# The closing stage of a mixer-and-experts kernel: its first load in two transfers, its last chunk finished in two halves

## The chip, the cores and the metric

The kernel runs on one core of one Trainium2 chip. The metric is the time of one execution on the device in microseconds (us), taken as the median of several runs. Profile views give times from the start of the span, which is the part of an execution that the profiler records.

## What is computed

One transformer-like layer on 4 x 1024 tokens of 256 values, in float32. First a sequence mixer with a residual, then a mixture of eight experts (two of them for each token, and a shared one), whose output is normalised and added to the mixer's result:

```python
x = x + _layernorm(attn_ref(_layernorm(x), ...))      # call the result x1
...
for e in range(E):
    out = out + comb[:, e:e + 1] * _swiglu(xn, gate_up_w[e], down_w[e])
out = out + _swiglu(xn, shared_gate_up_w, shared_down_w)
...
x = x + _layernorm(out)                               # x1 + normalised sums
```

The change concerns the last line only: for each of 4096 tokens, subtract the mean of its 256 sums, divide by the root of the variance plus 1e-5, and add x1.

## The kernel before

The mixer runs first, in `mixer`. It leaves three things in device memory: x1 in `x1_scratch`, each token's normalised row, sorted by expert, in `xs_scratch`, and the shared expert's output in `acc_scratch`. Then `experts` works through 39 groups of up to 256 token rows. For each group TensorE multiplies with the weights of its expert, which SyncE loads chunk by chunk, and GpSimd adds the results to `acc_scratch` with indirect DMAs that accumulate (L1271). When the last of these has landed, the closing stage begins. The expert phase takes most of the time; the closing stage starts at about 1162 of the span's 1199.7 us.

The closing stage handles the 4096 tokens in `NC` = 8 chunks of `TC` = 4 tiles of 128 tokens (512 KB each). The tiles `acc[c]` lie in buffers that the earlier stages no longer use: `xnt` for chunks 0 to 4, `x_in` for 5 and 6, and `s` for 7. The small statistics lie in `xr`. The work on a chunk passes through five engines in order:

- SyncE loads chunk after chunk from `acc_scratch` (L1255), all eight issues one behind the other.
- VectorE (`moments_of`) takes the statistics of the four tiles (`bn_stats`, L1462), aggregates them (L1467), and prepares the negative mean and the variance (L1470, L1471).
- GpSimd (`root`) raises the variance to the power of -1/2 and multiplies (L1281, L1283).
- ScalarE normalises each tile in place (L1396).
- Even chunks are stored by GpSimd with a DMA that adds to x1, which was copied into `out` before (`add_out`, L1289). For odd chunks VectorE adds x1 from on-chip memory (`add_x1`, L1477), and SyncE stores the sum (L1259).

The order on each engine is the order of the code. On VectorE, the x1 addition of an odd chunk comes two chunks late, so that its wait is short; that of chunk 7 comes last. On GpSimd, `add_out` of chunk c-2 comes behind `root(c)`, so the store of chunk 6 follows the root of chunk 7. SyncE waits for the loads' issue, then for `sum_ready` once for each odd chunk, and in the end for all stores, its own and GpSimd's:

```python
for c in range(1, NC, 2):
    sp.wait_ge(sum_ready, c // 2 + 1)
    sp.dma_start(token_rows(out)[c, :, :, :], acc[c]).then_inc(sum_stored, 16)
sp.wait_ge(sum_stored, 16 * (NC // 2))
sp.wait_ge(out_added, 16 * (NC // 2))
```

The semaphore `acc_loaded[c]` says that chunk c is loaded, and `normed` counts the chunks that ScalarE has normalised. SyncE's DMAs go through queue q1 (hardware_dynamic), GpSimd's through q0 (software_dynamic); both use the same 16 DMA engines.

Of the kernel before, what the change touches and what calls it, by code (L numbers as in the profile page):

```python
# [7 lines left out]
ALU = mybir.AluOpType  # L8
# [4 lines left out]
P = 128  # L13
# [1134 lines left out]
TC = 4  # L1148
NC = TT // TC


def token_rows(dram):

    return dram.rearrange("b l d -> (b l) d").rearrange("(c t p) d -> c p t d", t=TC, p=P)


def experts(nc, ctx, w_s, xs_dram, acc_dram, x1_dram, out, group_expert, group_change, group_row, group_code, vec, ident, neg_half,
# [5 lines left out]
    def sem(name):  # L1163
        return ctx.enter_context(nc.semaphore(name))

    LAG = 3
    w, rows, xg_hi, xg_lo, xg_f, gate, hg_hi, hg_lo, y, acc, x1, small = homes
# [9 lines left out]
    acc_loaded = [sem(f"f_loaded{c}") for c in range(NC)]  # L1177
    order, aggregated, moments = sem("f_order"), sem("f_aggregated"), sem("f_moments")
    rooted, rs_ready, normed = sem("f_rooted"), sem("f_rs_ready"), sem("f_normed")
    x1_moved, out_added = sem("x1_moved"), sem("out_added")  # L1180
    sum_ready, sum_stored = sem("sum_ready"), sem("sum_stored")

    gu_ps, down_ps, x_ps = banks[0:2], [banks[2:4], banks[4:6]], banks[6]
    loaded = [sem(f"chunk_loaded{f}") for f in range(FC)]
# [7 lines left out]
    def groups(eng, turn):  # L1192

        turn(0, 0)
        with eng.Fori(0, (NG - 1) // 2) as i:
            for k in range(2):
                turn(i * 2 + 1 + k, 1 - k)
# [3 lines left out]
    def sync(sp):  # L1201
        def load_rows(g, par):
            row = sp.value_load(group_row[0:1, bass.ds(g, 1)], min_val=0, max_val=SPARE)
            sp.dma_start(rows[:, par, :, :], xs_dram[bass.ds(row, G), :].rearrange("(t p) d -> p t d", p=P)
                         ).then_inc(rows_loaded[par], 16)

        def load_chunk(g, f, e, new):
            sp.wait_ge(down_done, g * FC + f + 1)
            sp.dma_start(w[f].bitcast(F32), w_s[e, f, :, :], cond=new).then_inc(loaded[f], 16)

        def turn(g, par):
            e = sp.value_load(group_expert[0:1, bass.ds(g, 1)], min_val=0, max_val=E - 1)
            new = sp.value_load(group_change[0:1, bass.ds(g, 1)], min_val=0, max_val=1)
            for f in range(FC):
                load_chunk(g, f, e, new)
                if f == 1:
                    if not (isinstance(g, int) and g == 0):
                        sp.wait_ge(x_turned, g * DC + DC)
                        sp.wait_ge(meta_ready, g)
                    load_rows(g + 1, 1 - par)  # L1220

        def first_rows(b, par=0):
            row = sp.value_load(star[0:1, 1 + par:2 + par], min_val=0, max_val=SPARE)
            sp.dma_start(rows[:, par, :, :], xs_dram[bass.ds(row, G), :].rearrange("(t p) d -> p t d", p=P)
                         ).then_inc(rows_loaded[par], 16)

        def first_weights():
            e = sp.value_load(star[0:1, 0:1], min_val=0, max_val=E - 1)
            for f in range(FC):
                sp.dma_start(w[f].bitcast(F32), w_s[e, f, :, :]).then_inc(loaded[f], 16)  # L1230

        def others():
            def move_x1(c):
                if c % 2 == 0:
                    sp.dma_start(token_rows(out)[c, :, :, :], token_rows(x1_dram)[c, :, :, :]).then_inc(x1_moved, 16)
                else:
                    sp.dma_start(x1[c // 2], token_rows(x1_dram)[c, :, :, :]).then_inc(x1_moved, 16)

            sp.wait_ge(x_turned, 2 * DC)
            sp.wait_ge(meta_ready, 1)  # L1240
            load_rows(2, 0)
            free(sp, "x1")
            move_x1(0)
            for c in range(1, NC):
                turn(c + 1, 1 - c % 2)
                move_x1(c)
            with sp.Fori(0, (NG - 1 - NC) // 2) as i:
                for k in range(2):
                    turn(i * 2 + NC + 1 + k, 1 - k)
            for par in range(2):  # L1250
                sp.wait_ge(rows_loaded[par], 16 * (NG // 2 + 1))
            for par in range(2):
                sp.wait_ge(y_added[par], 16 * GT * ((NG + 1 - par) // 2))
            for c in range(NC):
                sp.dma_start(acc[c], acc_dram[c * TC * P:(c + 1) * TC * P, :].rearrange("(t p) d -> p t d", p=P)  # L1255
                             ).then_inc(acc_loaded[c], 16)
            for c in range(1, NC, 2):
                sp.wait_ge(sum_ready, c // 2 + 1)
                sp.dma_start(token_rows(out)[c, :, :, :], acc[c]).then_inc(sum_stored, 16)  # L1259
            sp.wait_ge(sum_stored, 16 * (NC // 2))  # L1260
            sp.wait_ge(out_added, 16 * (NC // 2))
        return first_rows, first_weights, others

# [97 lines left out]
    def scalar(act):  # L1361
        def rows_hi(g, par, c):
            act.wait_ge(x_turned, g * DC + c + 1)
            nc.scalar.activation(xg_hi[:, par, c, :], x_ps[:, 0:G], ACT.Identity,
                                 bias=vec[:, V_BE + c:V_BE + c + 1],
                                 scale=vec[:, V_G + c:V_G + c + 1]).then_inc(x_hi_ready, 1)
            nc.scalar.activation(xg_f[:, c, :], x_ps[:, 0:G], ACT.Identity,
                                 bias=vec[:, V_BE + c:V_BE + c + 1],
                                 scale=vec[:, V_G + c:V_G + c + 1]).then_inc(x_f_ready, 1)

        def h_high(g, f):
            act.wait_ge(h_ready, g * FC + f + 1 + 2)
            nc.scalar.activation(hg_hi[:, f % 4, :], gate[:, f % 4, :], ACT.Copy).then_inc(h_hi_ready, 1)  # L1373
        def turn(g, par):
            for f in range(FC):
                if f >= 1:
                    h_high(g, f - 1)
                elif not (isinstance(g, int) and g == 0):
                    h_high(g - 1, FC - 1)
                act.wait_ge(clipped, g * FC + f + 1)  # L1380
                nc.scalar.activation(gate[:, f % 4, :], gate[:, f % 4, :], ACT.Silu).then_inc(silu_ready, 1)  # L1381
                if f in (2, 5):
                    rows_hi(g + 1, 1 - par, (f - 2) // 3)
        def first_hi(b, c):
            if c == 0:
                free(act, "xg")
            rows_hi(0, 0, c)

        def rest():
            act.sem_inc(down_done, FC)  # L1390
            groups(act, turn)
            h_high(NG - 1, FC - 1)
            for c in range(NC):
                act.wait_ge(rs_ready, c + 1)
                for t in range(TC):
                    i = nc.scalar.activation(acc[c][:, t, :], acc[c][:, t, :], ACT.Identity, bias=nm[:, c, t:t + 1],  # L1396
                                             scale=rs[:, c, t:t + 1])
                i.then_inc(normed, 1)
        return first_hi, rest

    def vector(dve):
# [52 lines left out]
        def rest():  # L1454
            free(dve, "gate")
            groups(dve, turn)
            h_low(NG - 1, FC - 1)
            copy_y(NG - 1, 0)
            def moments_of(c):
                dve.wait_ge(acc_loaded[c], 16)  # L1460
                for t in range(TC):
                    i = nc.vector.bn_stats(st[:, c, t, :], acc[c][:, t, :])  # L1462
                i.then_inc(order, 1)
                dve.wait_ge(order, c + 1)
                dve.sem_inc(seen, 1)
                for t in range(TC):
                    i = nc.vector.bn_aggr(mv[:, c, t, :], st[:, c, t, :])  # L1467
                i.then_inc(aggregated, 1)
                dve.wait_ge(aggregated, c + 1)
                nc.vector.tensor_scalar(mv[:, c, :, 0], mv[:, c, :, 0], -1.0, None, ALU.mult)  # L1470
                nc.vector.tensor_scalar(ve[:, c, :], mv[:, c, :, 1], 1.0, EPS, ALU.mult, ALU.add).then_inc(moments, 1)  # L1471

            def add_x1(c):
                if c == 1:
                    dve.wait_ge(x1_moved, 16 * NC)
                dve.wait_ge(normed, c + 1)
                nc.vector.tensor_tensor(acc[c], acc[c], x1[c // 2], ALU.add).then_inc(sum_ready, 1)  # L1477

            for c in range(NC):
                moments_of(c)  # L1480
                if c % 2 == 1 and c > 1:
                    add_x1(c - 2)
            add_x1(NC - 1)
        return seeds, first_lo, rest

    return sync, gpsimd, tensor, scalar, vector
# [69 lines left out]
```

## Time and profile before

| | us |
|---|---|
| median of 3 runs | 1206.18 |
| lowest and highest | 1205.74 and 1206.53 |
| the profiled execution, its own time | 1201.74 |
| its span | 1199.7 |
| TensorE busy in the span | 1106.7 (92%) |
| VectorE busy | 828.7 (69%) |
| ScalarE busy | 654.8 (55%) |
| GpSimd busy | 307.5 (26%) |

The profiled execution is one execution by itself, and what a view says of durations holds for it. Its time lies 2.0 us above its span and 4.4 us below the median of the runs. Busy shares are of the whole span, most of which is the mixer and the experts; the closing stage, where TensorE does nothing, must be read in stretches of its own.

### The profile page before, as it was taken

The numbers are of one execution on the slowest core, as the hardware profiler recorded it, in microseconds if no ns is written. First come the engines' busy times: TensorE is split into PE (matmuls) and PEld (weight loads), VectorE is DVE, ScalarE is ACT, GpSimd is POOL, SyncE is SP. The second block draws the span as 40 slices with busy tenths as digits, with TensorE's granted clock in tenths as the row PEclk, the third lists the DMA queues.
The fourth block names the chain that finished last, engine by engine and source line by source line (L and its number), as shares of the span: only waits on it lengthen the run. The fifth ranks groups of instructions, "written<-read, shape, count | busy, mean of one in ns | idle before, by whom it ended". The sixth has DMA issues, their size and how long they took to land.

```text
span 1199.7 us, 23250 instructions
## 1 busy us (share of the span) xinstructions
PE 1106.7 (92%) x7492; PEld 981.8 (82%) x7492; DVE 828.7 (69%) x2089; ACT 654.8 (55%) x1304; POOL 307.5 (26%) x358
## 2 busy tenths in 40 slices
PE   4899899999989999999999999999999999999950
PEld 2665676676677567999999999999999999999940
DVE  4896888798797666666666666666666666666645
ACT  6777768677685354444444444444444444444425
POOL 2032032722542634121221122112112211221225
PEclk9899999999999999999999999999999999999985
DMA  8657675875675678532231245555912356211239
GB/s 275 224 195 235 224 226 191 271 256 175 231 248 174 212 246 339 147 70 54 53 70 20 33 137 184 187 173 180 367 33 35 77 202 229 35 25 28 35 79 219
DMA packets 96617, 191.70 MB, mean 160 GB/s; under 512 B 8768, under 2 KB 59456, under 8 KB 96576
## 3 DMA queue, kind: packets, MB, share of 16 engines
q1 hardware_dynamic: 80160, 170.38, 41.8%
q0 software_dynamic: 16416, 20.85, 10.2%
q8 instruction: 17, 0.28, 0.1%
q14 instruction: 24, 0.20, 0.1%
HBM read 295.62 MB, written 86.41 MB: 318 GB/s over the span
## 4 chain that ended last, share of the span: by engine, by line
PE 81%; DVE 5%; ACT 4%; issue 4%; DMA 3%; POOL 3%; SPq 1%; ACTq 0%; DVEq 0%; POOLq 0%
PE bank L1321 12%; PE bank L1322 12%; PE bank L1323 12%; PE bank L457 11%; PE bank L1334 6%; PE bank L1332 6%; PE bank L1333 6%; PE bank L451 4%; PE bank L453 4%; PE bank L452 4%; POOL xs_scratch L1128 2%; PE bank L1309 1%; DMA xs_scratch<-n,slot_now 1%; DVE xr L1462 1%; PE bank L468 1%
## 5 line engine op out<-in xcount | busy, mean ns | idle before, releaser
L1271 POOL DMA_INDIRECT acc_scratch<-cv,ids x78 | 128.2, 1644 | 559.6 <-DVE cv L1410 518.6
L1321 PE MATMUL bank<-h_hi,w_both 128*128 128x256 f32 x936 | 269.9, 288 | 0.4 <-DVE cv L1438 0.4
L1431 DVE TENSOR_SCALAR cv<-bank 128x256 f32<-128x256 f32 x312 | 132.2, 424 | 198.7 <-PE bank L1323 197.9
L1322 PE MATMUL bank<-h_hi,w_both 128*128 128x256 f32 x936 | 262.9, 281 | 0.0
L1323 PE MATMUL bank<-h_hi,w_both 128*128 128x256 f32 x936 | 262.2, 280 | 0.0
L1381 ACT ACTIVATE cv<-cv 128x256 f32<-128x256 f32 x312 | 130.3, 418 | 241.4 <-DVE cv L1431 240.4
L1373 ACT ACTIVATE h_hi<-cv 128x256 fp32r<-128x256 f32 x312 | 129.7, 416 | 115.0 <-DVE cv L1438 115.0
L1321 PEld LDWEIGHTS bank<-h_hi,w_both 128*128 128x128 f32 x936 | 176.5, 189 | 0.7 <-issue 0.7
L1323 PEld LDWEIGHTS bank<-h_hi,w_both 128*128 128x128 f32 x936 | 176.8, 189 | 0.0
L1322 PEld LDWEIGHTS bank<-h_hi,w_both 128*128 128x128 f32 x936 | 176.5, 189 | 0.0
L1438 DVE TENSOR_TENSOR cv<-bank,cv 128x256 f32<-128x256 f32 x312 | 132.5, 425 | 46.9 <-ACT cv L1381 40.2
L1333 PE MATMUL bank<-w_both,h_hi 128*128 128x256 f32 x468 | 132.0, 282 | 0.0
L1334 PE MATMUL bank<-w_both,h_hi 128*128 128x256 f32 x468 | 131.9, 282 | 0.0
L1332 PE MATMUL bank<-w_both,h_hi 128*128 128x256 f32 x468 | 131.8, 282 | 0.0
L1426 DVE TENSOR_TENSOR h_hi<-cv,h_hi 128x256 fp32r<-128x256 f32 x312 | 130.2, 417 | 0.8 <-ACT h_hi L1373 0.6
L451 PE MATMUL bank<-xs_hi,w_both 128*128 128x512 f32 x224 | 99.2, 443 | 17.7 <-DVE xs_lo L825 10.4
L1111 POOL TENSOR_TENSOR h_lo<-h,h_hi 128x512 fp32r<-128x512 f32 x32 | 47.3, 1483 | 171.7 <-ACT h_hi L706 171.7
L453 PE MATMUL bank<-xs_hi,w_both 128*128 128x512 f32 x224 | 90.4, 404 | 0.0
L452 PE MATMUL bank<-xs_lo,w_both 128*128 128x512 f32 x224 | 90.4, 404 | 0.0
L1334 PEld LDWEIGHTS bank<-w_both,h_hi 128*128 128x128 f32 x468 | 88.4, 189 | 0.0
L1333 PEld LDWEIGHTS bank<-w_both,h_hi 128*128 128x128 f32 x468 | 88.1, 188 | 0.0
L1332 PEld LDWEIGHTS bank<-w_both,h_hi 128*128 128x128 f32 x468 | 87.8, 188 | 0.0
(227 smaller groups left out, 2405.3 us busy)
## 6 DMA issues: line engine op xcount, KB each, us to landing
w_both<-w_split SPq DMA_DIRECT2D x228, 768.0 KB
xs_hi<-w_split SPq DMA_DIRECT2D x38, 768.0 KB
xs_lo<-w_split SPq DMA_DIRECT2D x38, 768.0 KB
e_raw<-w_e SPq DMA_DIRECT2D x64, 384.0 KB
w_split<-e_high SPq DMA_DIRECT2D x64, 384.0 KB
w_split<-e_raw SPq DMA_DIRECT2D x64, 384.0 KB
u<-xs_scratch SPq DMA_DIRECT2D x40, 260.0 KB, 3.4
x_in<-x SPq DMA_DIRECT2D x8, 512.0 KB, 5.6
```

The source lines that it names most:

```text
L451: nc.tensor.matmul(out, hi, x_hi, start=first, stop=False)
L452: nc.tensor.matmul(out, hi, x_lo, start=False, stop=False)
L453: return nc.tensor.matmul(out, lo, x_hi, start=False, stop=last)
L457: return nc.tensor.matmul(out, w, x, start=first, stop=last)
L1321: nc.tensor.matmul(out, e_hi[f][:, cols], xg_hi[:, par, c, :], start=c == 0, stop=False)
L1322: nc.tensor.matmul(out, e_hi[f][:, cols], xg_lo[:, par, c, :], start=False, stop=False)
L1323: i = nc.tensor.matmul(out, e_lo[f][:, cols], xg_hi[:, par, c, :], start=False, stop=c == DC - 1)
L1332: nc.tensor.matmul(out, hg_hi[:, f % 4, toks], e_hi[f][:, 4 * P:CW], start=f == 0, stop=False)
L1333: nc.tensor.matmul(out, hg_hi[:, f % 4, toks], e_lo[f][:, 4 * P:CW], start=False, stop=False)
L1334: i = nc.tensor.matmul(out, hg_lo[:, f % 4, toks], e_hi[f][:, 4 * P:CW], start=False, stop=f == FC - 1)
L1431: nc.vector.tensor_scalar(gate[:, f % 4, :], gu_ps[f % 2][:, 0:G], CLIP, -CLIP, ALU.min, ALU.max).then_inc(clipped, 1)
L1438: nc.vector.tensor_tensor(gate[:, f % 4, :], gu_ps[f % 2][:, G:2 * G], gate[:, f % 4, :], ALU.mult).then_inc(h_ready, 1)
```

## The change

The first load becomes two transfers of 256 KB, each for two of the four tiles. The first one signals a new semaphore, `acc_half_loaded`, the second one `acc_loaded[0]`. VectorE starts on the first two tiles after the first signal and waits for the second ahead of the third tile. On the last chunk, ScalarE also signals `normed` after its second tile; VectorE adds x1 to two tiles at a time, and SyncE stores each half when it is ready. The other six chunks, and the statistics and roots of all, are as before.

```diff
--- before.py
+++ after.py
@@ -1179,6 +1179,8 @@
     rooted, rs_ready, normed = sem("f_rooted"), sem("f_rs_ready"), sem("f_normed")
     x1_moved, out_added = sem("x1_moved"), sem("out_added")
     sum_ready, sum_stored = sem("sum_ready"), sem("sum_stored")
+    acc_half_loaded = sem("acc_half_loaded")
+    TH = TC // 2
 
     gu_ps, down_ps, x_ps = banks[0:2], [banks[2:4], banks[4:6]], banks[6]
     loaded = [sem(f"chunk_loaded{f}") for f in range(FC)]
@@ -1251,13 +1253,20 @@
                 sp.wait_ge(rows_loaded[par], 16 * (NG // 2 + 1))
             for par in range(2):
                 sp.wait_ge(y_added[par], 16 * GT * ((NG + 1 - par) // 2))
-            for c in range(NC):
+            first_rows_of_acc = acc_dram[0:TC * P, :].rearrange("(t p) d -> p t d", p=P)
+            sp.dma_start(acc[0][:, 0:TH, :], first_rows_of_acc[:, 0:TH, :]).then_inc(acc_half_loaded, 16)
+            sp.dma_start(acc[0][:, TH:TC, :], first_rows_of_acc[:, TH:TC, :]).then_inc(acc_loaded[0], 16)
+            for c in range(1, NC):
                 sp.dma_start(acc[c], acc_dram[c * TC * P:(c + 1) * TC * P, :].rearrange("(t p) d -> p t d", p=P)
                              ).then_inc(acc_loaded[c], 16)
-            for c in range(1, NC, 2):
+            for c in range(1, NC - 1, 2):
                 sp.wait_ge(sum_ready, c // 2 + 1)
                 sp.dma_start(token_rows(out)[c, :, :, :], acc[c]).then_inc(sum_stored, 16)
-            sp.wait_ge(sum_stored, 16 * (NC // 2))
+            for h in range(2):
+                half = slice(h * TH, (h + 1) * TH)
+                sp.wait_ge(sum_ready, NC // 2 + h)
+                sp.dma_start(token_rows(out)[NC - 1, :, half, :], acc[NC - 1][:, half, :]).then_inc(sum_stored, 16)
+            sp.wait_ge(sum_stored, 16 * (NC // 2 + 1))
             sp.wait_ge(out_added, 16 * (NC // 2))
         return first_rows, first_weights, others
 
@@ -1395,6 +1404,8 @@
                 for t in range(TC):
                     i = nc.scalar.activation(acc[c][:, t, :], acc[c][:, t, :], ACT.Identity, bias=nm[:, c, t:t + 1],
                                              scale=rs[:, c, t:t + 1])
+                    if c == NC - 1 and t == TH - 1:
+                        i.then_inc(normed, 1)
                 i.then_inc(normed, 1)
         return first_hi, rest
 
@@ -1457,8 +1468,10 @@
             h_low(NG - 1, FC - 1)
             copy_y(NG - 1, 0)
             def moments_of(c):
-                dve.wait_ge(acc_loaded[c], 16)
+                dve.wait_ge(acc_half_loaded if c == 0 else acc_loaded[c], 16)
                 for t in range(TC):
+                    if c == 0 and t == TH:
+                        dve.wait_ge(acc_loaded[0], 16)
                     i = nc.vector.bn_stats(st[:, c, t, :], acc[c][:, t, :])
                 i.then_inc(order, 1)
                 dve.wait_ge(order, c + 1)
@@ -1480,7 +1493,11 @@
                 moments_of(c)
                 if c % 2 == 1 and c > 1:
                     add_x1(c - 2)
-            add_x1(NC - 1)
+            for h in range(2):
+                half = slice(h * TH, (h + 1) * TH)
+                dve.wait_ge(normed, NC + h)
+                nc.vector.tensor_tensor(acc[NC - 1][:, half, :], acc[NC - 1][:, half, :], x1[NC // 2 - 1][:, half, :],
+                                        ALU.add).then_inc(sum_ready, 1)
         return seeds, first_lo, rest
 
     return sync, gpsimd, tensor, scalar, vector
```

On SyncE, the closing stage before. The first row waits for everything ahead of the stage; the last waits for all stores.

```order
L1255 DMA xnt<-acc_scratch 128x4x256 [waits y_added0,y_added1,x_rows_loaded1,x_rows_loaded0]
L1255 DMA xnt<-acc_scratch 128x4x256 x4
L1255 DMA x_in<-acc_scratch 128x4x256 x2
L1255 DMA s<-acc_scratch 128x4x256
L1259 DMA out<-xnt 128x4x256 [waits sum_ready] x2
L1259 DMA out<-x_in 128x4x256 [waits sum_ready]
L1259 DMA out<-s 128x4x256 [waits sum_ready]
L64 UNCONDITIONAL_BRANCH [waits out_added,sum_stored]
```

And on SyncE now:

```order
L1257 DMA xnt<-acc_scratch 128x2x256 [waits y_added0,y_added1,x_rows_loaded1,x_rows_loaded0]
L1258 DMA xnt<-acc_scratch 128x2x256
L1260 DMA xnt<-acc_scratch 128x4x256 x4
L1260 DMA x_in<-acc_scratch 128x4x256 x2
L1260 DMA s<-acc_scratch 128x4x256
L1264 DMA out<-xnt 128x4x256 [waits sum_ready] x2
L1264 DMA out<-x_in 128x4x256 [waits sum_ready]
L1268 DMA out<-s 128x2x256 [waits sum_ready] x2
L64 UNCONDITIONAL_BRANCH [waits out_added,sum_stored]
```

There is one more load ahead of the seven that follow, and one more store at the end; all the others keep their places.

On VectorE, the first chunk of the stage before, behind the last two results of the experts (L1410):

```order
L1410 TENSOR_SCALAR cv<-bank,share 128x256
L1462 BN_STATS xr<-xnt 128x6 [waits f_loaded0]
L1462 BN_STATS xr<-xnt 128x6 x3
L1467 BN_AGGR xr<-xr 128x2 [waits f_order]
L1467 BN_AGGR xr<-xr 128x2 x3
```

The same place now:

```order
L1421 TENSOR_SCALAR cv<-bank,share 128x256
L1475 BN_STATS xr<-xnt 128x6 [waits acc_half_loaded]
L1475 BN_STATS xr<-xnt 128x6
L1475 BN_STATS xr<-xnt 128x6 [waits f_loaded0]
L1475 BN_STATS xr<-xnt 128x6
L1480 BN_AGGR xr<-xr 128x2 [waits f_order]
L1480 BN_AGGR xr<-xr 128x2 x3
```

The four statistics have two waits instead of one. At the end of the stage, VectorE's last row `L1477 TENSOR_TENSOR` on 128x1024 values has become two of `L1499` on 128x512, each with a wait for `normed`. No instruction of ScalarE or GpSimd has moved.

## Rows read from the trace of the kernel before

**Rows 1.** Chain of waits that ended last, stretch 1140:1200 (start us, us, what)

```profile
1162.64 4.14 DMA xnt<-acc_scratch
```

**Rows 2.** Timeline, stretch 1150:1200 (start us, us, engine, line, operation [idle before, releaser])

```profile
1166.81 1.41 DVE L1462 BATCH_NORM_STATS2 xr<-xnt 128x6 f32<-128x256 f32 x4 [10.79 <-DMA xnt<-acc_scratch]
...
1168.91 1.40 DVE L1462 BATCH_NORM_STATS2 xr<-xnt 128x6 f32<-128x256 f32 x4
...
1185.30 1.34 POOL L1289 DMA_DIRECT2D out<-xnt  x1
...
1186.24 0.39 DVE L1471 TENSOR_SCALAR xr<-xr 128x4 f32<-128x4 f32 x1
...
1187.56 0.37 SPq L1259 DMA_DIRECT2D out<-x_in  x1
...
1188.72 1.34 POOL L1289 DMA_DIRECT2D out<-x_in  x1
1188.73 2.07 ACT L1396 ACTIVATE s<-s,xr 128x256 f32<-128x256 f32 x4 [1.34 <-POOL xr L1283]
1190.84 1.23 DVE L1477 TENSOR_TENSOR s<-s,e_high 128x1024 f32<-128x1024 f32 x1 [3.31 <-ACT s L1396]
1192.09 0.37 SPq L1259 DMA_DIRECT2D out<-s  x1
```

**Rows 3.** DMA queues (packets, MB, share), the five stretches that the prediction names, in order

```profile
q1 hardware_dynamic: 4072, 4.04, 108.6%
...
q0 software_dynamic: 334, 0.34, 113.2%
...
q1 hardware_dynamic: 188, 0.19, 108.1%
...
q0 software_dynamic: 322, 0.33, 114.1%
...
q1 hardware_dynamic: 373, 0.37, 69.0%
```

**Rows 4.** Times to landing, lines L1289, L1259: chunks 3, 4, 5, 6, 7, by start

```profile
L1259 SPq DMA_DIRECT2D out<-xnt x1: 378/378/378, 1181.8 to 1181.8; - x1
...
DMA to landing us min/median/max: 6.3/6.3/6.3
...
DMA to landing us min/median/max: 6.0/6.0/6.0
...
DMA to landing us min/median/max: 5.4/5.4/5.4
...
DMA to landing us min/median/max: 7.0/7.0/7.0
...
DMA to landing us min/median/max: 5.0/5.0/5.0
```

**Rows 5.** Line L64, the program's end: the drains of GpSimd and SyncE

```profile
L64 POOLq DRAIN  x1: 10741/10741/10741, 1188.7 to 1188.7; - x1
...
L64 SPq DRAIN  x1: 7/7/7, 1197.2 to 1197.2; - x1
```

**Rows 6.** Line L1255, load of chunk 1; line L1396, chunk 7 (ns, start us)

```profile
L1255 SPq DMA_DIRECT2D xnt<-acc_scratch x1: 501/501/501, 1163.1 to 1163.1; - x1
...
DMA to landing us min/median/max: 5.2/5.2/5.2
...
L1396 ACT ACTIVATE s<-s,xr x4: 585/586/600, 1188.7 to 1190.2; 128x256 f32<-128x256 f32 x4
```

**Rows 7.** Queue, stretch 1162.6:1165; then stretches: busy by engine, clock, DMA share, GB/s

```profile
q1 hardware_dynamic: 137, 0.14, 35.3%
...
1165.25:1165.50 0.25, 0.00 (x0) 0.00 (x0) 0.00 (x0) 0.00 (x0) 0.00 (x0) 0.50 1.10 393
...
1188.00:1188.50 0.50, 0.00 (x0) 0.00 (x0) 0.00 (x0) 0.00 (x0) 0.42 (x2) 0.50 0.93 121
1188.50:1189.00 0.50, 0.00 (x0) 0.00 (x0) 0.00 (x0) 0.27 (x1) 0.48 (x2) 0.50 1.15 184
```

## Prediction

> **What bounds the closing stage.** I read three views. First the chain of waits that ended last [rows 1]: the stage began with a 4.14 us wait for the first 512 KB load of the sums, and from there the chain ran over VectorE. Then the timeline [rows 2], which shows why: VectorE started the statistics of chunk 0 at 1166.81, those of chunk 1 at 1168.91, and worked through all eight chunks nearly without a pause, to 1186.63 (the 0.39 us instruction that began at 1186.24). It waits for data only once, the 10.79 us ahead of chunk 0. So what chunk 0 gains, the rows behind it can gain too, as far as their own loads have landed.
>
> After 1186.63 the page's chain goes GpSimd root, ScalarE normalising, VectorE add, SyncE store, and stops at the add that ends at 1192.07. The span is 1199.7. What fills the 7.6 us in between is in neither view; it has to be read from the queues [rows 3]. There each queue has a stretch to itself. In 1188.0:1190.0 all 334 packets are on q0 (GpSimd's accumulating stores), in 1191:1191.5 all 188 are on q1 (SyncE's plain stores), in 1192.6:1194.4 all 322 are on q0 again, and in 1195.5:1197 all 373 are on q1. With the landings [rows 4] this gives an order. Chunk 4 (GpSimd, issued 1185.30, 6.0 us) landed at 1191.3; chunk 5 (SyncE, 1187.56, 5.4) at 1192.9; chunk 6 (GpSimd, 1188.72, 7.0) at 1195.7; chunk 7 (SyncE, 1192.09, 5.0) at 1197.1. The engines serve one store, then the next, and the last four are a backlog: chunk 5, issued at 1187.56, moved nothing in 1188.0:1190.0, and chunk 7, issued at 1192.09, moved nothing in 1192.6:1194.4. **The end of the kernel hangs on the DMA engines, not on the last add.** What feeds this backlog is the issue of chunk 4 at 1185.30.
>
> Behind that lies one more step [rows 5]: GpSimd's closing drain began at 1188.7 and took 10741 ns, so it ended at 1199.5, about 3.8 us after chunk 6 landed and 2.4 us after chunk 7 landed; SyncE's own drain took 7 ns, at 1197.2. The program ends when GpSimd's drain does. That the last plain store is on the end path is therefore not even certain.
>
> **Part 1, the first load in two transfers.** SyncE issues one more load; the one for chunk 1 took 0.50 us [rows 6]. The loads behind it come up to 0.5 us later to the queue but not later to the engines: from 1165 on, q1 moved 4072 packets of about 1 KB by 1176.5 at 351 GB/s [rows 3], so the bytes, not the issues, set when each load lands. I cost the issue at nothing; if that cover is gone, it costs its 0.5 us. Of the 512 packets of chunk 0, the second 256 take 262 KB / 393 GB/s = 0.67 us by the rate at which the stream ran in 1165.25:1165.50 [rows 7]. So the first half should land 0.67 us earlier, at 1166.1 instead of 1166.78. VectorE then does two of the four statistics (1.41 / 4 each, 0.71 together) while the rest lands, and the aggregates come 0.7 earlier. Now what is late next: the load of chunk 1, issued at 1163.1, landed 5.2 us later [rows 6], at 1168.3. VectorE could now ask for it at 1168.2 and waits until about 1168.32, against 1168.91 before. **Gain 0.59 us.** Chunk 2's load follows by 512 KB / 351 GB/s = 1.5 us, at 1169.8, well ahead of 1168.32 + 2.1 (the distance of the two rows of statistics) = 1170.4, when VectorE asks for it. Bounds: 0, if the two half transfers do not land in order; 0.71, if the stream itself starts sooner because its first transfer is shorter (from 1162.6 to 1165 only 137 packets moved [rows 7]). I take 0.59, the row of chunk 1.
>
> This moves every root, normalisation and store issue by 0.59, GpSimd's issue of chunk 4 too. Does the backlog follow? GpSimd's store of chunk 4 reached its full rate only at about 1188.4, 3.1 us after its issue (121 GB/s in 1188.0:1188.5, then 184 [rows 7]); chunk 3 (SyncE, 1181.8, 6.3) had landed at 1188.1 [rows 4]. So chunk 4's rate rose when both its own start and chunk 3 were over, and its own start was the later by a little. I let the whole of the 0.59 through, and keep 0 as the lower end, for the case that the engines, busy from 1165 on, simply stay full of the same bytes.
>
> **Part 2, the last chunk in two halves.** The four ScalarE passes of 586 ns [rows 6] take 2.07 us together [rows 2], so they start (2.07 - 0.59) / 3 = 0.49 us apart. The first two are done at 1188.73 + 0.49 + 0.59 = 1189.81, the first half add (1.23 / 2 = 0.62) at 1190.43, the second at 1190.84 + 0.62 = 1191.46, and the second half store issues 0.6 us before 1192.09. On the issue side that is 0.6 us; the extra SyncE issue (0.37) lies in an idle queue, and nothing is queued behind either wait. But chunk 7 then stands behind chunk 6 anyway, which held the engines until shortly before 1195.5 [rows 3]. **Gain 0.** Its bounds: +0.6, were the issue what counts, and a loss, below. The extra completions and the extra increments cost nothing I can see on an engine that has anything waiting.
>
> A rule of the Trainium skill reads this otherwise: "DMA: Bandwidth & Descriptors", section Anatomy of one DMA, fits a transfer as about 2.0 us plus bytes over 436 GB/s, which would be 2.6 us for the last half store and would let part 2 pay in full; its outcome is the first rival below. No run here shows it for this store: rows 4 have 5.0 us for 512 KB, because of the queue.
>
> **Sum**: 0.59 + 0 = 0.6 us off the profiled execution's 1201.74. The median of the runs, 1206.18, lies 4.4 us above that execution; the stage is a fixed piece at the end, so I take the same difference off it: 1205.6. About 0.2% (2.4 us) is what a measurement of this kernel can tell from no change, and the forecast is a quarter of that.
>
> **The rivals.**
> *Both parts pay.* The end follows the issue of the last store, as the chain of waits [rows 1] alone would suggest: 0.59 + 0.61 = 1.2 us, 1205.0. Against it stands the silence of q1 in 1192.6:1194.4. Chance 0.15.
> *Nothing moves.* Either the half loads land together, or the DMA engines keep the same finish because they are never short of work: 1206.2. For it: q1 and q0 together leave no empty stretch in rows 3. Against: the slow starts of GpSimd's stores. Chance 0.27.
> *The last store's halves overtake chunk 6.* This is the one that ends slower. Half A would be issued at about 1189.9 and half B at 1190.9, while chunk 5, on the same q1, is still being served until about 1191.5. If the engines stay with q1 while it has work, A and B (0.67 us each) go ahead of chunk 6, which had landed at 1195.7; GpSimd's drain, which ends 3.8 us behind that landing [rows 4, 5], goes with it. With A alone and part 1's gain: +0.67 - 0.59 = +0.1. With A and B: +1.34 - 0.59 = +0.75, 1206.9; without part 1's gain +1.34, 1207.5. It decides from the point at which half A is ready before chunk 5 is done, about 1191.5. Against it: chunk 6, issued on q0 while q1's chunk 5 was waiting or running, was served next, but no q1 work competed then, so the rows leave it open. Chance 0.13.
> The Trainium skill's "DMA: Bandwidth & Descriptors", section Queues, rings and completion order, has the engines take turns between queues at packet boundaries, typically 9 to 17 descriptors. By that rule half A would share with chunk 6 rather than wait, and delay it by up to its own length, a case that lies between the two prices above. The trace shows no such sharing between whole stores, which put 32 pieces on each engine.
> *The forecast*, part 1 alone: 0.45.
>
> **Range and chances.** All the cases lie between 1205.0 and 1207.5. The three runs before spread by 0.8 us, so I add half of that at each end, and leave out the far end of the last rival: 1204.5 to 1207.1. None of the cases reaches 2.4 us. What is left for faster or slower is a shift that no row shows, such as a median that settles elsewhere (the profiled execution is itself 4.4 us from it): faster 0.05, within 0.2% 0.91, slower 0.04.
>
> **What would show it.** Step 1: VectorE's first statistics start at about 1166.1 after the same start of the loads (3.5 us behind the first issue rather than 4.2), the second two without a wait over 0.1, and a new wait of about 0.1 us at chunk 1. Chunk 4's store issues 0.6 us earlier relative to the first load. Step 2: two half adds of 0.6 us, two stores of 256 KB on SyncE, and still no q1 packets for most of chunk 6's service; both halves land within 0.7 us of each other. End: GpSimd's drain ends 3.8 us behind chunk 6's landing, and last. I am wrong if the last half lands before chunk 6 does, if chunk 6's time to landing grows from 7.0 us by more than the 0.1 or so of noise between rows, or if the drain ends at 10.74 us after its own start whatever lands when.

## The result, and the profile after

The changed kernel takes 1209.37 us in the median of 20 runs, the kernel before 1206.43 us in the median of 20. The ratio is 1.0023, with a 95% interval of 1.0012 to 1.0034: the change costs about 2.8 us, between 1.4 and 4.1. Two of the 20 executions before, of 3925.51 and 6275.7 us, say nothing of the kernel; without them its median is 1206.26. 1205.6 had been forecast, with a range of 1204.5 to 1207.1.

The profiled execution of the changed kernel, 1212.7 us, is the longest of its 20, and most of its distance from the one before lies ahead of the change: its closing stage begins 8.5 us later. So the stage is measured by itself, from the issue of its first load to the end of the span. Before it was 1199.7 - 1162.64 = 37.06 us; now it is 1210.6 - 1171.15 = 39.45 us. That is 2.4 us more, close to what the medians say. The timeline of the stage shows both parts of the change at work [rows 2] (start us, us, engine, line, operation; in brackets the idle time before and what ended it):

```profile
1171.15 0.38 SPq L1257 DMA_DIRECT2D xnt<-acc_scratch  x1
1171.58 0.46 SPq L1258 DMA_DIRECT2D xnt<-acc_scratch  x1
...
1174.01 1.47 DVE L1475 BATCH_NORM_STATS2 xr<-xnt 128x6 f32<-128x256 f32 x4 [9.50 <-DMA xnt<-acc_scratch]
...
1178.56 1.41 DVE L1475 BATCH_NORM_STATS2 xr<-xnt 128x6 f32<-128x256 f32 x4 [2.30 <-DMA xnt<-acc_scratch]
...
1198.39 1.34 POOL L1298 DMA_DIRECT2D out<-x_in  x1
1198.40 2.08 ACT L1405 ACTIVATE s<-s,xr 128x256 f32<-128x256 f32 x4 [1.34 <-POOL xr L1292]
1199.53 0.69 DVE L1499 TENSOR_TENSOR s<-s,e_high 128x512 f32<-128x512 f32 x1 [2.32 <-ACT s L1405]
1200.25 1.35 SPq L1268 DMA_DIRECT2D out<-s  x2
1200.51 0.69 DVE L1499 TENSOR_TENSOR s<-s,e_high 128x512 f32<-128x512 f32 x1 [0.29 <-ACT s L1405]
```

The first statistics start 2.86 us behind the first issue instead of 4.17, a gain of 1.3 us, and the second pair of them waits for nothing. Then VectorE stands still for 2.30 us until chunk 1 has landed, a wait that was not there before. Chunk 1's statistics start 7.41 us behind the first issue instead of 6.27: 1.14 us lost. From there to GpSimd's issue of chunk 6 nothing changed: 19.8 us both times. The half adds and the issues of the half stores come, relative to that of chunk 6, within 0.15 us of where the prediction had them.

The landings of chunk 1, chunk 6, and the two halves of chunk 7, each under its issue, complete the picture (duration of the issue in ns, its start; then us to landing) [rows 4, 6]:

```profile
L1260 SPq DMA_DIRECT2D xnt<-acc_scratch x1: 471/471/471, 1172.1 to 1172.1; - x1
DMA to landing us min/median/max: 6.5/6.5/6.5
...
L1298 POOL DMA_DIRECT2D out<-x_in x1: 1336/1336/1336, 1198.4 to 1198.4; - x1
DMA to landing us min/median/max: 8.3/8.3/8.3
...
L1268 SPq DMA_DIRECT2D out<-s x1: 373/373/373, 1200.2 to 1200.2; - x1
DMA to landing us min/median/max: 5.6/5.6/5.6
...
L1268 SPq DMA_DIRECT2D out<-s x1: 372/372/372, 1201.2 to 1201.2; - x1
DMA to landing us min/median/max: 6.1/6.1/6.1
```

Chunk 1 takes 6.5 us to land instead of 5.2, and chunk 6's accumulating store 8.3 us instead of 7.0. The queues in 1203:1205, in the middle of chunk 6's store, tell why the latter [rows 3]. Before, all 322 packets of such a stretch were on q0; now the half stores run beside them:

```profile
q0 software_dynamic: 255, 0.26, 80.4%
q1 hardware_dynamic: 211, 0.21, 38.3%
```

GpSimd's closing drain became longer by the same 1.3 us [rows 5], and it still ends the program:

```profile
L64 POOLq DRAIN  x1: 12028/12028/12028, 1198.4 to 1198.4; - x1
...
L64 SPq DRAIN  x1: 7/7/7, 1207.5 to 1207.5; - x1
```

So the 2.4 us are 1.1 at the loads and 1.3 at the last store. The stretches around the late load show a hole in the stream (stretch, us, busy time of the five engines, TensorE's clock, DMA share, GB/s) [rows 7]:

```profile
1173.50:1174.00 0.50, 0.00 (x0) 0.00 (x0) 0.00 (x0) 0.00 (x0) 0.00 (x0) 0.50 0.98 344
1174.00:1174.50 0.50, 0.00 (x0) 0.00 (x0) 0.49 (x2) 0.00 (x0) 0.00 (x0) 0.50 0.52 168
1174.50:1175.00 0.50, 0.00 (x0) 0.00 (x0) 0.50 (x2) 0.00 (x0) 0.00 (x0) 0.50 0.48 147
...
1177.00:1177.50 0.50, 0.00 (x0) 0.00 (x0) 0.00 (x0) 0.00 (x0) 0.42 (x2) 0.50 1.00 338
```

The DMA engines were busy half the time for 1.5 us, from 2.9 us behind the first issue on, while more loads stood in the queue. Before, the stream ran at about 340 GB/s or more from 2.4 us on, without a hole.

### The profile page after: what moved, and what is told of

It is laid out like the page before. It is cut to its first block, busy times and chain, and to the rows that moved or that the text cites. A ratio compares the mean times of both kernels' runs of the same rounds, so it can differ in the third digit from the quotient of the medians.

```text
span 1210.6 us, 23253 instructions
## 1 busy us (share of the span) xinstructions
PE 1111.1 (92%) x7492; PEld 986.9 (82%) x7492; DVE 829.5 (69%) x2090; ACT 654.7 (54%) x1304; POOL 305.5 (25%) x358
## 4 chain that ended last, share of the span: by engine, by line
PE 79%; DVE 5%; ACT 4%; issue 3%; POOL 3%; DMA 2%; SPq 1%; another core or an unknown queue 1%; ACTq 0%; DVEq 0%; POOLq 0%
PE bank L1330 12%; PE bank L1331 12%; PE bank L1332 12%; PE bank L457 9%; PE bank L1343 6%; PE bank L1341 6%; PE bank L1342 6%; PE bank L451 4%; PE bank L453 4%; PE bank L452 4%; POOL xs_scratch L1128 2%; PE bank L1318 1%; DMA xs_scratch<-n,slot_now 1%; DVE xr L1475 1%
## 5 line engine op out<-in xcount | busy, mean ns | idle before, releaser
L451 PE MATMUL bank<-xs_hi,w_both 128*128 128x512 f32 x224 | 101.0, 451 | 17.7 <-DVE xs_lo L825 10.4
L453 PE MATMUL bank<-xs_hi,w_both 128*128 128x512 f32 x224 | 91.5, 409 | 0.0
```

Of the source, the lines that this page charges most:

```text
L451: nc.tensor.matmul(out, hi, x_hi, start=first, stop=False)
L453: return nc.tensor.matmul(out, lo, x_hi, start=False, stop=last)
```

## The experiments

The numbers compared below are the length of the closing stage, VectorE's start on chunk 1 and chunk 6's time to landing. The kernel before, profiled again, gives their spread. The runs were made on four chips, on which the whole kernel takes between 1196 and 1207 us; each ratio is to the kernel before on the same chip, while the lengths of the stage are compared across chips. A run without a ratio is one execution. The letters of the theories are those of the expectations shown ahead of each result.

**One part alone, and the kernel before again.** `load_only` keeps the split load and takes the other edits back; `tail_only` is the reverse. `before_again` is the kernel before.

> The first load in two transfers, the last chunk whole as before. Measure: the closing stage, from the issue of the first load to the end of the span, 37.0 us in the profile before and 39.4 with the whole change. Theory S (the small transfers leave the engines short of work behind them): the statistics start about 2.8 us after the first issue, but chunk 1 lands about 7.4 us after it instead of 5.7, VectorE waits about 2.3 us for it, and the stage takes about 38.1 us, 1.1 more than before. Rival C (the gap in the load stream was an accident of that one execution): chunk 1 lands by 5.7 us and the stage takes 36.4 us. Median time: S about 1 us above before, C about 0.6 below.

> The first load whole, the last chunk finished in two halves. Theory I (the half stores come into GpSimd's last store and share its engines): chunk 6 takes about 8.3 us to land instead of 7.0, q1 and q0 both carry packets in that stretch, GpSimd's drain takes about 12.0 us instead of 10.7 and the stage about 38.3 us against 37.0. Rival L (the sharing came only from the shifted order behind the late loads): chunk 6 lands in 7.0 us as before, the drain takes 10.7 and the stage 37.0. Median time: I about 1.3 us above before, L the same.

> The kernel before, profiled once more, to see how far the closing stage repeats. If the gap in the loads is an accident, it may show here too; if it belongs to the small transfers, the stage takes 37.0 us within 0.2, chunk 1 lands about 5.7 us after the first issue and chunk 6's store in about 7.0 us.

`load_only` took a ratio of 1.0005 (0.9991 to 1.0020) to the kernel before, `tail_only` 1.0018 (1.0006 to 1.0030); their excesses add up to the 1.0023 of the whole, though each interval is as wide as that. `before_again` had no hole, chunk 1 in by 5.4 us, chunk 6 in 6.9 us and a stage of 36.7 us, so the stage repeats within 0.4 us, somewhat more than I had allowed. `tail_only` confirms theory I in kind: chunk 6 took 7.9 us, and the stage 37.8 us. In the ten profiles in which no store of chunk 7 ran beside it for long, chunk 6 took 6.8 to 7.4 us, so 7.9 lies outside, if not by much. The queues in 1192:1193.5 of its profile, and its drain:

```profile
q0 software_dynamic: 185, 0.19, 78.0%
q1 hardware_dynamic: 156, 0.16, 38.9%
...
L64 POOLq DRAIN  x1: 11622/11622/11622, 1187.6 to 1187.6; - x1
```

`load_only` has the hole, but a shorter one. Its first load was issued at 1159.10:

```profile
1161.84 1.49 DVE L1469 BATCH_NORM_STATS2 xr<-xnt 128x6 f32<-128x256 f32 x4 [9.35 <-DMA xnt<-acc_scratch]
...
1165.46 1.41 DVE L1469 BATCH_NORM_STATS2 xr<-xnt 128x6 f32<-128x256 f32 x4 [1.34 <-DMA xnt<-acc_scratch]
```

Chunk 1 starts 6.36 us behind the first issue, and the stage takes 36.9 us. The hole is thus not an accident of one execution, and its cost varies; here it cost nothing against the kernel before. Theory S had the mechanism and too high a price, C neither.

**Is it VectorE's early reading?** In `one_wait` VectorE waits for both halves before its first statistics; the transfers are the same (the diff is against `load_only`).

```diff
-                dve.wait_ge(acc_half_loaded if c == 0 else acc_loaded[c], 16)
+                if c == 0:
+                    dve.wait_ge(acc_half_loaded, 16)
+                dve.wait_ge(acc_loaded[c], 16)
                 for t in range(TC):
-                    if c == 0 and t == TH:
-                        dve.wait_ge(acc_loaded[0], 16)
```

> The first load in two transfers, but VectorE waits for both before the first statistics; the last chunk whole. It tells the stream of loads from the earlier start of the statistics. Theory S: chunk 1 still lands about 7.4 us after the first issue, since the stream is set by the transfers alone. Rival V (VectorE's early reading of chunk 0 slows the loads that run beside it): chunk 1 lands by about 5.7 us again. Stage: S about 38.1 us, V about 36.6.

Chunk 1's statistics began at 7.49 us, after a wait of 1.75 us, and the stage took 38.0 us. V has fallen: the hole belongs to the transfers.

**Does the drain decide, and does sharing delay it?** `hold` is `tail_only` with one more wait of SyncE's ahead of each half store; `whole_early` leaves out the addition of x1 to chunk 7, so that it can store that chunk whole straight after its normalisation, earlier than any kernel with the right output could.

```diff
                 sp.wait_ge(sum_ready, NC // 2 + h)
+                sp.wait_ge(out_added, 16 * (NC // 2))
```

```diff
-                sp.wait_ge(sum_ready, c // 2 + 1)
+                if c == NC - 1:
+                    sp.wait_ge(normed, NC)
+                else:
+                    sp.wait_ge(sum_ready, c // 2 + 1)
...
-            add_x1(NC - 1)
```

> The last chunk in two halves as in the change, the load whole, and SyncE lets both half stores wait until all of GpSimd's stores have landed. Theory I (the half stores slow GpSimd's last store, and its drain, 3.77 us behind that landing, ends the kernel): chunk 6 lands in 6.9 to 7.0 us again, the drain takes 10.7 us, and the stage is 36.7 to 37.1 us, although the last half is issued some 4 us later than in the change. Rival E (the end follows the last landing on SyncE's queue): the stage grows by the later issue, to about 38.5 us or more.

> The kernel before, but chunk 7 is stored whole straight after its normalisation, without the addition of x1 to it (left out, so that the store can be issued early): about 28.0 us after the first load's issue, between the 27.9 and 28.9 of the two half stores. Theory N (what lets a store share the engines with GpSimd's is that it is small): no packet of chunk 7 moves until chunk 6's are nearly all done, chunk 6 lands in 7.0 us, the drain takes 10.7 us. Rival T (what matters is that it is issued early): it shares as the halves do, chunk 6 takes about 8 us, the drain 11.6 us or more.

`hold` issued its halves at 32.9 and 33.4 us, about 5 us later than `tail_only`. Chunk 6 again took 6.9 us, and the stage was 36.85 us, 1.0 less than in `tail_only`. A last store that is issued almost 5 us later ends the kernel 1 us sooner: E has fallen. Each half, with the engines to itself, landed in 2.2 to 2.4 us. Its drain, and behind it that of `whole_early`:

```profile
L64 POOLq DRAIN  x1: 10654/10654/10654, 1189.9 to 1189.9; - x1
```

```profile
L64 POOLq DRAIN  x1: 11985/11985/11985, 1182.3 to 1182.3; - x1
```

`whole_early` gave T, where I had leaned to N: issued at 28.1 us, the whole store shared the engines with chunk 6 as the halves do (in 1187.5:1189, below), chunk 6 took 8.2 us and the stage 38.2.

```profile
q0 software_dynamic: 179, 0.18, 74.0%
q1 hardware_dynamic: 186, 0.19, 43.8%
```

So it is not the size of the last store that does the harm but its early issue, which the halves bring about. In the kernel before it was issued at 29.5 us, and its first packets came only when chunk 6's were ending.

What lets a store share is not settled by this. Chunk 1's store in the kernel before was issued at 1176.49, before GpSimd's store of chunk 0 had moved a packet, and still it waited. The first stretch is 1176.5:1176.8, with the last packets of the loads, the second 1177:1179.7:

```profile
q1 hardware_dynamic: 15, 0.01, 13.5%
...
q0 software_dynamic: 419, 0.43, 114.3%
```

**A cure for the tail.** GpSimd's accumulating stores are slow (183 GB/s in 1192.6:1194.4 of the kernel before, where SyncE's had 385 in 1191:1191.5), and the drain waits for the last of them. `g_plain` gives chunk 6 to VectorE and SyncE as well. Its x1 is loaded into the mixer's tile `g`, which is idle by then. `g_halves` does so on top of `tail_only`.

```diff
+        x1_spare = by_tile(flat(g[:, :, :]))
...
-            for c in range(1, NC, 2):
-                sp.wait_ge(sum_ready, c // 2 + 1)
+            for k, c in enumerate(list(range(1, NC - 1, 2)) + [NC - 2, NC - 1]):
+                sp.wait_ge(sum_ready, k + 1)
...
-            add_out(NC - 2)
...
+            add_x1(NC - 2)
             add_x1(NC - 1)
```

> The kernel before, with x1 of chunk 6 also held on chip, so that VectorE adds it and SyncE stores it; GpSimd's last store is then that of chunk 4. Theory D (drain 3.77 us behind GpSimd's last landing, and the slow accumulating store holds up what follows): GpSimd's drain ends at about 32.2 us, no longer last; chunk 6 lands at about 31.3, chunk 7, issued at 29.2, in about 4 us at 33.2, and the stage takes about 33.6 us, 3.2 less than before. Rival F (the closing takes some fixed time whatever queue is last): SyncE's last landing at 33.2 is followed by the 2.5 us seen before, 35.7.

> As g_plain, and the last chunk in two halves as in the change. With no store of GpSimd's beside them, theory I has the halves pay: the second half is issued at about 28.9 us and lands in about 3 us, 31.9, so GpSimd's drain (32.2) and SyncE's landing nearly meet and the stage takes about 32.5 us. Rival W (small transfers are slow by themselves, or stand behind chunk 6's plain store): the second half lands at 33 or later, and the stage is no shorter than 33.6. Median time: about 4.3 us below before by I, about 3 by W.

> The same kernel as g_plain, timed: whether the 4.2 us that its closing stage is shorter (32.66 us against 36.67 to 37.06) stand in the median. By the drain theory the median is 3.8 to 4.4 us below before, as for g_halves (4.6 there), and the stage again 32.6 us; if the halves were worth something by themselves, g_plain stays above g_halves by more than 1 us.

`g_plain` has a stage of 32.7 us, 4.0 to 4.4 less than the two profiles of the kernel before, and chunk 7, without chunk 6's slow store ahead of it, lands 3.0 us after its issue instead of 5.0. The drain now ends first, and the program ends 0.2 us behind SyncE's, so F has fallen:

```profile
L64 POOLq DRAIN  x1: 6077/6077/6077, 1189.7 to 1189.7; - x1
...
L64 SPq DRAIN  x1: 7/7/7, 1196.5 to 1196.5; - x1
```

`g_halves` has the same 32.7 us. That is about what theory I gave for it, but `g_plain` has it too, 0.9 us below its own forecast: the last half lands at 32.3 us, as the whole store of `g_plain` does. The halves pay nothing even without a slow store beside them, which is W's point, though not W's numbers. The second profile of `g_plain`, that of `g_plain_timed`, has 33.0 us. Timed against the kernel before, `g_halves` has a ratio of 0.9962 (0.9948 to 0.9975) and `g_plain` 0.9968 (0.9952 to 0.9984). The intervals overlap. Both are faster than the kernel before, and so than the changed one at 1.0023; `g_plain` does it with no splitting at all.

**The hole in the loads.** Four more kernels change only the loads: all eight in halves, the first two, the second alone, and the first half issued by ScalarE instead of SyncE. A fifth is `load_only` once more. `HALVED` is 8 in `all_halved` and 2 in `two_halved`; `second_halved` has `if c == 1` there and one wait; `act_first` is the second diff, against `load_only`.

```diff
+                if c < HALVED:
+                    first = acc_half_loaded if c == 0 else acc_loaded[c]
+                    sp.dma_start(acc[c][:, 0:TH, :], rows_of_acc[:, 0:TH, :]).then_inc(first, 16)
+                    sp.dma_start(acc[c][:, TH:TC, :], rows_of_acc[:, TH:TC, :]).then_inc(acc_loaded[c], 16)
```

```diff
-            sp.dma_start(acc[0][:, 0:TH, :], first_rows_of_acc[:, 0:TH, :]).then_inc(acc_half_loaded, 16)
...
+            for par in range(2):
+                act.wait_ge(y_added[par], 16 * GT * ((NG + 1 - par) // 2))
+            act.dma_start(acc[0][:, 0:TH, :], first_rows_of_acc[:, 0:TH, :]).then_inc(acc_half_loaded, 16)
```

> All eight loads in two transfers of 256 KB (chunk 0 with two waits as in the change, the others with one for both), the last chunk whole. Theory G (the gap comes where a whole transfer stands behind small ones: the small ones reach the engines sooner and are through before the first whole one is ready): no gap, q1 moves about 350 GB/s from 1.5 us on, chunk 1 lands by about 5.2 us behind the first issue and VectorE does not wait for it, all loads are through by about 13.8 us; stage about 35.6 us. Rival H (small transfers cost the engines something each): the stream stays below 340 GB/s, the last load lands at 15 us or later, and chunk 1 later than 6 us; stage 37 us or more.

> Chunks 0 and 1 in two transfers each, the rest whole; the last chunk whole. By theory G the gap moves behind chunk 1, to about 4.5 us after the first issue, where VectorE is still busy with chunks 0 and 1, so that chunk 2 (needed at about 7 us) may come 0.5 us late or in time: stage 36.0 to 36.7 us. By rival H it is spread over both, chunk 1 lands later than 6 us, stage 37 us or more.

> Chunk 0 loaded whole, chunk 1 in two transfers (one wait for both), the rest whole, the last chunk whole. Theory Z (the gap comes from an early first transfer: the engines start on a half at 1.5 us instead of 2.3 us behind the first issue and run out of prepared work at about 3 us): no gap, q1 above 340 GB/s from 2.5 us on, chunk 1 in by 5.7 us, stage 36.7 to 37.1. Rival H (a small transfer leaves a gap behind it wherever it stands): a gap at about 4 to 6 us, VectorE waits for chunk 2 or the last load lands later than 14.7 us.

> Chunk 0 in two halves with two waits as in the change, but the first half is issued by ScalarE, through its own queue, at the same time as SyncE issues the second half; the last chunk whole. Theory Z (the engines outrun the queue's preparation of transfers; two queues prepare more): the gap at 3.0 us is gone or smaller, chunk 1 lands by about 5.7 us, stage 36.2 to 36.7 us. Rival Q (the gap does not come from one queue's preparation): a gap as in load_only, chunk 1 asked for at about 5.1 us and in at 6.3 or later, stage 36.9 or more.

> load_only once more. In three executions with this stream of loads VectorE began chunk 1 at 6.36, 7.41 and 7.49 us behind the first issue. Theory Z and rival H both have the gap again; the question is its size: a start of chunk 1 between 6.3 and 7.5 us would say that the gap is always there and its length is what varies, a start at 5.2 us or so that it comes in some executions only.

| kernel | GB/s at 3.0 to 4.0 us | VectorE starts chunk 1 | stage |
|---|---|---|---|
| before | 388 | 6.27 | 37.1 |
| before_again | 381 | 6.05 | 36.7 |
| after | 141 | 7.41 | 39.4, the tail included |
| load_only | 213 | 6.36 | 36.9 |
| load_again | 216 | 6.35 | 37.3 |
| one_wait | 154 | 7.49 | 38.0 |
| all_halved | 208 | 5.92 | 37.1 |
| two_halved | 90 | 7.88 | 38.9 |
| second_halved | 382 | 6.28 | 37.2 |
| act_first | 383 | 5.78 | 36.6 |

Times are us behind the stage's first issue. `load_again` has the hole once more, with the same start of chunk 1 as `load_only`. `all_halved` has it too, with no whole transfer in the stream, and `two_halved` has the deepest one, at the same place and not behind chunk 1. So G, which put the hole where a whole transfer follows small ones, has fallen.

H, a gap behind any small transfer, is not out. Both have the stage of 37 us or more that it gave them, and chunk 1 came late in `two_halved`. In `all_halved` the last load landed at 15.5 us, as H had it, but in `load_only`, with seven whole loads, it landed at 15.4, and the stream of `all_halved` recovered to between 287 and 326 GB/s at 4 to 6 us and to 338 and more from then on. With the first load whole (`second_halved`) the stream ran at 380 GB/s until 4 us, as Z had it, and chunk 1 came in time. But it fell to 262 GB/s at 5.0 to 5.5 us, behind the small transfers, and the last load landed at 14.8 us, which is H again; nobody waited for it. H does not say why two small chunks do more harm than eight, and `act_first` speaks against it, since SyncE's own 256 KB transfer there left no gap.

With the first half on a queue of its own (`act_first`) there was no hole:

```profile
1156.13 0.47 ACTq L1400 DMA_DIRECT2D xnt<-acc_scratch  x1
1156.25 0.38 SPq L1257 DMA_DIRECT2D xnt<-acc_scratch  x1
...
1159.81 1.41 DVE L1472 BATCH_NORM_STATS2 xr<-xnt 128x6 f32<-128x256 f32 x4 [10.16 <-DMA xnt<-acc_scratch]
...
1161.91 1.40 DVE L1472 BATCH_NORM_STATS2 xr<-xnt 128x6 f32<-128x256 f32 x4
```

But the engines then pass 300 GB/s only 3.0 us behind the first issue, later than with whole loads, and the first statistics start at 3.68 us, not 2.8, so that most of the early start is gone too. Q has fallen as it stands, but the run took away the early start together with the single queue, and cannot tell which of them the hole needs. Its stage, 36.6 us, is 0.1 to 0.5 us below the kernel before, from one execution, which is no more than the 0.4 us by which the stage repeats.

What can be said is this: in all six profiles in which SyncE issues a first load of 256 KB, the engines pass 300 GB/s at about 1.8 us instead of 2.3, and fall to a mean of 90 to 216 GB/s at 3.0 to 4.0 us; none of the others does. The fall begins at about 2.8 us, when just chunk 0's 512 packets have been moved: in the kernel with the change 467 packets from 0.5 to 2.75 us and 527 by 3.0 us. That they start on small transfers before the queue has prepared enough of what follows fits this and `act_first`, but would not by itself make `two_halved` the worst or give the later dip of `second_halved`, and it was not measured. The cause of the hole, and of its varying length, stays open.

## Why the prediction was wrong, point by point

*What bounds the stage.* That GpSimd's drain ends the program, 3.8 us behind chunk 6's landing, was right: from 35.5 to 39.3 us now and from 32.9 to 36.6 in `hold`. In `g_plain`, where the landing is that of chunk 4, the drain follows it by the same distance, from 28.0 to 31.7, and no longer ends the program. That the drain might take 10.74 us whatever lands, the last of the signs of being wrong, has fallen. That "the engines serve one store, then the next" failed. I took the silence of q1 beside chunk 6 for a rule of the engines. In the kernel before, chunk 7's packets began 2.7 us behind its issue, when chunk 6's were nearly through; in `whole_early` they began 2.4 us behind an issue 1.3 us sooner, in the middle of chunk 6's.

*Part 1, +0.59 us.* The first step was undersized: the first half landed 2.8 us behind the first issue, and the first statistics came 1.3 us earlier, not 0.7. The step that failed is "the bytes, not the issues, set when each load lands", on which the landing of chunk 1 at 1168.3 and the lower bound of 0 rested. The stream of the kernel before ran at 351 GB/s whatever was issued, but that was a stream of whole transfers. With two small ones ahead it fell to 141 GB/s at 3.0 to 4.0 us, and chunk 1 landed 7.4 us behind the first issue instead of 5.7. In place of a gain of 0.59 us stands a loss of 1.14 us in this profile. In the three others with the change's loads the stage took 36.9, 37.3 and 38.0 us (the last without the early statistics) against 36.7 and 37.1; by the medians `load_only` loses 0.6 us, with an interval that holds zero.

*Part 2, 0.* That the halves gain nothing was right, and the step to their issue was near: the last half store issues 0.5 us earlier than the whole one did, counted from the statistics of chunk 1, and 0.6 were worked out. That they cost nothing failed. The third rival, given a chance of 0.13, is what happened, in its weaker form: the halves do not go ahead of chunk 6 but share with it. Its prices ran from 0.67 to 1.34 us without the gain of part 1; measured are 1.3 us here and 0.9 in `tail_only` (7.9 us against 7.0), and 2.2 us in the ratio of its timed runs (0.7 to 3.6). One of the signs of being wrong came with it, a time to landing of chunk 6 that grew by more than 0.1 us, and the halves landed 1.5 us apart, not within 0.7. The argument that set its chance was the same reading of q1's silence. The rule of the Trainium skill's "DMA: Bandwidth & Descriptors", section Queues, rings and completion order, that an engine goes round the queues it has work for, was put beside this rival, and the trace agrees with it once both queues have work: 255 packets on q0 and 211 on q1 in one stretch. By itself it does not tell why chunks 1 and 3 of the kernel before, issued beside a store of GpSimd's, moved nothing for 3.3 to 3.5 us, until that store was ending.

*The first rival's estimate.* The 2.6 us for a half store that stand beside it come from the Trainium skill's "DMA: Bandwidth & Descriptors", section Anatomy of one DMA, whose fit is for transfers that GpSimd issues. The half stores are SyncE's. They took 5.6 and 6.1 us in the change, beside chunk 6, and 2.2 and 2.4 us in `hold`, by themselves.

*The rivals.* "Both parts pay" and "nothing moves" are out. The sum failed on both terms, and since my lower bound for part 1 was 0, the range could not hold the result. Part 2's forecast replaced by the rival's 1.34 us, with part 1 at 0, gives 1207.5, the end that I had cut off. The hole's 1.14 us, and the 0.25 us by which the median before came out higher than the 1206.18 I had started from, bring it to 1208.9; the 0.5 us left lie within the interval. The range was also narrower than its own rule: half of 0.8 us on either side of the cases gives 1204.6 to 1207.3, or to 1207.9 with the far end kept, and the result lies outside all of these.

## What to carry to other kernels

Ask of a transfer that is to start earlier what it will run beside: a store issued 1.3 us sooner delayed the slower store on which the end hung, and holding the halves back gave the lost time back, though no more. A steady stream in a trace tells what that sequence of transfers does, not what another one will do, so the bounds on a split of its first piece must reach into a loss. And find out what the last step of a program waits for before shortening anything ahead of it: here it was GpSimd's last accumulating store, and moving that one chunk to a plain store brought about 4 us, some seven times what halving had been hoped to.

## What the runs showed of the hardware that I had not expected

GpSimd's closing drain ended 3.7 to 3.8 us behind the landing of its last store, in every kernel; SyncE's took 7 ns. A store of 512 KB issued by SyncE 2.1 us behind GpSimd's of the chunk ahead ran beside it at 246 GB/s in all (the half stores at 232 and 235), where q1 alone had 385 and q0 alone 183; issued 1.3 us later it came after it. That early issue is not the whole condition, as chunk 1 shows, and which one it is stays open. And a first load of 256 KB on SyncE's queue, which landed in 2.6 to 2.9 us, was followed by a hole in the stream of the loads behind it, 90 to 216 GB/s at 3.0 to 4.0 us where whole loads have 381 and more, in six of six profiles; no hole appeared when ScalarE's queue carried it, in one.
